# Two graph layers on one core: one block for both layers, closed blocks of new x among the last sums, and more rows fetched one by one

## The reference, cut to what matters

```python
h = maximum(layernorm(x), 0)
# layer 0: attention over the edges of each receiver, 4 heads of 32 channels
y = h @ W + b_lin
logit = leaky_relu(sum over (sent | received) channels of feat * alpha)   # per edge and head
att = exp(logit - max of the receiver) ; att = att / sum of the receiver
x = x + segment_sum(att * y[src], dst) + bias
h = maximum(layernorm(x), 0)
# layer 1: messages
ef  = (relu(edge_attr @ We1 + be1) @ We2 + be2) * sigmoid(ts @ Wt + bt)
msg = relu([h[src] | ef] @ Wn1 + bn1) @ Wn2 + bn2
x = x + (segment_sum(msg, dst) + h)
```

## Time and profile before

| | us |
|---|---|
| median of 3 runs (lowest, highest) | 2124.97 (2122.21, 2127.07) |
| the profiled execution's own time | 2122.82 |
| its span | 2121.0 |
| layer 0 from the start to the meeting of the engines | about 1055.7 |
| new x, to the first gather of layer 1 | 1055.7 to 1089.5 |
| layer 1 | 1089.5 to 2121.0 |

### The profile page before, as it was taken

The page is one execution under the profiler, slowest core; times in us unless marked ns, Lnnn a source line. Parts: engine busy times, 40 slices in busy tenths (PEclk is TensorE's granted clock), DMA queues, the critical chain, the costliest instruction groups (busy, mean ns, idle before and its releaser), DMA issues.

```text
span 2121.0 us, 47035 instructions
## 1 busy us (share of the span) xinstructions
PE 1524.8 (72%) x8785; PEld 1051.5 (50%) x8785; DVE 1461.3 (69%) x5237; ACT 929.9 (44%) x2818; POOL 1563.2 (74%) x1660
## 2 busy tenths in 40 slices
PE   6556555555555454454658998989989898898888
PEld 5434444444444343343545665656555555555556
DVE  8676767676766566565786886777767676666667
ACT  8535253535353342442466444444434443444343
POOL 7777777777777777777277777777777777777775
PEclk9766666666666666566679999999989999999999
DMA  7222222222222222222063544545544444454453
GB/s 203 54 57 57 57 57 57 58 57 57 57 58 57 56 58 57 57 56 54 22 184 107 144 144 144 145 123 146 150 128 144 144 145 144 119 146 138 133 151 105
DMA packets 111001, 213.56 MB, mean 101 GB/s; under 512 B 35214, under 2 KB 74350, under 8 KB 100723
## 3 DMA queue, kind: packets, MB, share of 16 engines
q0 software_dynamic: 51968, 107.32, 19.1%
q1 hardware_dynamic: 53031, 101.47, 16.2%
q10 hardware_dynamic: 5708, 1.77, 0.4%
HBM read 197.54 MB, written 12.88 MB: 99 GB/s over the span
## 4 chain that ended last, share of the span: by engine, by line
POOL 26%; issue 11%; PE 6%; DVE 5%; DMA 2%; ACT 1%; DVEq 1%; ACTq 0%; POOLq 0%; SPq 0%
POOL acc L1044 26%; DMA acc<-table,index 2%; PE pair L1122 1%; DVE acc L1392 1%; PE bank L1131 1%; PE pair L1116 1%; PE bank L1142 1%; DVE onehot L1350 1%; DVE pre L1374 1%; DVE ef L1357 1%; DVE x_rows L1288 0%; ACTq L1239 0%; PE bank L1073 0%; ACT msg L1223 0%; ACT hidden L1210 0%
## 5 line engine op out<-in xcount | busy, mean ns | idle before, releaser
L1044 POOL DMA_INDIRECT acc<-table,index x812 | 770.2, 949 | 252.5 <-issue 242.3
L356 POOL DMA_INDIRECT rows<-table,index x764 | 726.5, 951 | 233.0 <-issue 228.4
L812 ACT ACTIVATE rows<-rows,edge_w 128x32 f32<-128x32 f32 x1626 | 351.9, 313 | 1.1 <-issue 0.4
L504 DVE TENSOR_TENSOR acc<-acc,pair 128x256 f32 x832 | 349.2, 420 | 3.9 <-issue 2.5
L499 DVE TENSOR_SCALAR onehot<-iota_row,dst_rel 128x128 f32<-128x128 f32 x832 | 252.0, 304 | 135.2 <-PE pair L675 103.8
L1392 DVE TENSOR_TENSOR acc<-acc,bank 128x128 f32 x832 | 239.0, 287 | 143.5 <-issue 35.7
L675 PE MATMUL pair<-onehot,rows 128*128 128x128 f32 x1626 | 334.2, 367 | 0.5 <-ACT rows L812 0.5
L675 PEld LDWEIGHTS pair<-onehot,rows 128*128 128x128 f32 x1626 | 285.7, 264 | 58.9 <-issue 30.3
L1210 ACT ACTIVATE hidden<-pair,be 128x512 f32<-128x512 f32 x208 | 142.9, 687 | 380.0 <-PE pair L1122 172.4
L1131 PEld LDWEIGHTS bank<-wn1b,ef 128*128 128x128 f32 x1664 | 232.1, 202 | 109.7 <-issue 104.0
L1116 PE MATMUL pair<-ea,we 64*128 64x512 f32 x416 | 243.9, 668 | 42.4 <-DMA ea<-in_ea_t 42.4
(11 more groups left out here) (168 smaller groups left out, 1207.9 us busy)
## 6 DMA issues: line engine op xcount, KB each, us to landing
ts<-in_ts SPq DMA_DIRECT2D x52, 1024.0 KB
rows_x<-table SPq DMA_DIRECT2D x1664, 0.5 KB
ea<-in_ea_t SPq DMA_DIRECT2D x52, 512.0 KB, 5.0
rows_y<-table SPq DMA_DIRECT2D x1664, 0.5 KB
acc<-table,index POOLq DMA_INDIRECT x812
moments<-table ACTq DMA_DIRECT2D x768, 0.5 KB
rows_z<-table ACTq DMA_DIRECT2D x768, 0.5 KB
rows<-table,index POOLq DMA_INDIRECT x764
```

The source lines that it names most:

```text
L356: gp.indirect_dma_start(rows0[:, n % (RING * TG), :], None, table1, bass.IndirectOffsetOnAxis(index[:, n:n + 1], 0)).then_inc(half_in[g % ...
L504: dve.tensor_tensor(acc2[:, :, ds(v, P)], acc2[:, :, ds(v, P)], both_sums[n // TG % 2][:, :, n % TG * P:(n % TG + 1) * P], ALU.add).then_i ...
L812: act.activation(row, row, ACT.Copy, scale=edge_w[:, r % 2, (g - SPANS[r][0]) * TG + t, h:h + 1]).then_inc(scaled0, 1)
L1044: gp.indirect_dma_start(rows[:, g % RG1, t, :], None, table, bass.IndirectOffsetOnAxis(index[:, n:n + 1], 0)).then_inc(gathered[g % RG1], 16)
```

## The change

1. The two blocks become one: each engine runs its layer 0 program and goes on with its layer 1 program, without a meeting. The nodes are taken in the 13 parts that layer 1 closes them in (`CUTS`: one part per group from 195 on), in two stages: parts 0 to 8 (closed by group 203) and 9 to 12.
2. New x among the last sums: PE turns the statistics of closed parts during span 25 and the sums during span 26; DVE's statistics, shares, `scaled_sums` and `mix` stand between the last additions. POOL's own term now comes after `mix`, and SP writes a part to `table3` after the own term. PSUM banks 6 and 7 are freed for it (penalties, ends, carries and weights share bank 5). Tables of this step lie in slots of the ring of rows.
3. The maxima of span 26 are made within span 25 one group earlier (3, 4, 5, 6 for 4, 5, 6, 7). In every span `turn_penalties` stands after group 1 on PE and `keep_row_penalties` after group 2 on DVE (0 and 1 before).
4. SP fetches 15 tiles in layer 0 (groups 20, 33, ..., 189, a step of 13, and then 204) and the 10 rows of tile 830, for which `keep_logits` of span 26 waits too (`tail_in`); in layer 1 14 tiles (groups 21, 35, ..., 203, `LINE_STEP` 14) and the 10 rows of tile 830, ahead of the last `load`.
5. In SP's program the weights of layer 1 and `load(0)`, `load(1)` now come after the writes of `table3`.

The diff without the lines that only lose their indentation, cut:

```diff
-LINE_TILES = [g * TG for g in range(28, GROUPS, 14)]
-LINE_STEP = 15
+LINE_TILES = [g * TG for g in [*range(20, GROUPS - RG - HALF, 13), GROUPS - HALF]]
+LINE_STEP = 14
-EMPTY = range(-(-E // P), TILES)
+SHORT = E // P
+EMPTY = range(SHORT, TILES)
+LAST, CLOSE = TURNS - 1, TURNS - 2
+STAGES = [0, SPANS[LAST][0] - FIRST_END, PARTS]
...
-                return (4, 5, 6, 7) if r == TURNS - 1 else ()
+                return (3, 4, 5, 6) if r == LAST else ()
...
     # SyncE, layer 0
                     for j in range(len(LINE_TILES)):
                         line(j)
+                sp.wait_ge(agg0, SHORT // TG - RING + 1)
+                for o in range(0, E % P, BATCH):
+                    fill = min(BATCH, E % P - o)
+                    sp.load(regs[0:fill], line_index[0:1, len(LINE_TILES) * P + o:len(LINE_TILES) * P + o + fill])
+                    for q, v in enumerate(regs[0:fill]):
+                        row = sp.snap(v, min_val=0, max_val=N - 1)
+                        sp.dma_start(rows0[o + q:o + q + 1, SHORT % (RING * TG), :], table1[ds(row, 1), :]).then_inc(tail_in, 16)
                     sp.wait_ge(w2_in, 32)
+                for u in range(PARTS):
+                    sp.wait_ge(own, u + 1)
+                    sp.dma_start(table3[CUTS[u] * P:CUTS[u + 1] * P, :].rearrange("(b p) c -> p b c", p=P), x_rows[:, blocks_of(u), :]).then_inc(x1_out, 16)
...
     # ScalarE
                     def keep_logits(r):
+                    if r == LAST:
+                        act.wait_ge(tail_in, 16 * (E % P))
...
     # GpSimd, after the gathers of layer 0
+                for u in range(STAGES[1]):
+                    own_product(u)
+                for u in range(STAGES[1]):
+                    own_term(u)
+                for u in range(STAGES[1], PARTS):
+                    own_product(u)
+                for u in range(STAGES[1], PARTS):
+                    own_term(u)
...
     # VectorE, span 25 and then span 26
+                for k, g in enumerate(groups(CLOSE)):
+                    sum_group(g, at[k % HALF * TG:(k % HALF + 1) * TG])
+                    if k == logits_at:
+                        scan_rows(LAST)
+                    if k == ends_at:
+                        scan_row_ends(LAST)
+                    if k == carries_at:
+                        full_maxima(LAST)
+                    if k >= 1:
+                        gather_stats(k - 1)
+                gather_stats(7)
+                gather_stats(8)
+                maxima_of(0)
+                rescale(LAST, at)
+                shares(0)
+                sum_group(g1, at[0:TG])
+                scaled_sums(0)
+                sum_group(g1 + 1, at[TG:2 * TG])
+                scaled_sums(1)
+                mix(0)
+                add(n, at[2 * TG])
+                scaled_sums(2)
+                add(n + 1, at[2 * TG + 1])
+                mix(1)
...
+                gather_stats(12)
+                maxima_of(1)
+                scaled_sums(4)
+                shares(1)
+                scaled_sums(5)
+                mix(4)
...
+                scaled_sums(12)
+                mix(11)
+                mix(12)
...
     # SyncE, layer 1
+                def tail():
+                    sp.wait_ge(radd, SHORT // TG - RG1 + 1)
...
                     for q in range(loaded, GROUPS // HALF):
+                    if q == GROUPS // HALF - 1:
+                        tail()
                         load(q)
```

More of the change, by code:

```diff
@@ L22 @@
 UNITS = -(-NB // UB)
-EARLY = 3
 TG = 4
@@ L44 @@
 RAW_TURNS = 2
+WCOL = 4 * SH * (RT + 2)
+CARRY = WCOL + 2 * SH * (RT + 2)
 RAW = sum(SPAN_SIZES[:RAW_TURNS]) * TG
@@ L66 @@
 assert all(0 < y - x <= TG for x, y in zip(CUTS, CUTS[1:]))
+LAST, CLOSE = TURNS - 1, TURNS - 2
+STAGES = [0, SPANS[LAST][0] - FIRST_END, PARTS]
+assert STAGES == [0, 9, 13] and SPANS[CLOSE][1] == RG
+PART_SLOTS = 4
 ACT_ROWS = 4
@@ L234, in gnn_layers, with blocks_of, spread_of, heads @@
             act_index0_in = sem("act_index0_in")
+            sw_t, b_chain, e_in, e_done, s_t, cb_ready, ca_ready, owned, own, sums_kept, parted, mixed, count_kept, tail_in = (
+                sem(n) for n in ("sw_t", "b_chain", "e_in", "e_done", "s_t", "cb_ready", "ca_ready", "owned", "own", "sums_kept", "parted", "mixed",
+                                 "count_kept", "tail_in"))
+            def blocks_of(u):
+                return slice(CUTS[u], CUTS[u + 1])
+            def spread_of(u):
+                return CUTS[u + 1] - CUTS[u]
+            def heads(v):
+                return v.rearrange("p b (h c) -> p b h c", c=HC)
+            def per_head(v, u, n):
+                return v[:, blocks_of(u), 0:n].unsqueeze(3).broadcast_to([P, spread_of(u), n, HC])
+            def block_rows(b, u):
+                return b[:, 0:spread_of(u) * P].rearrange("p (m c) -> p m c", c=CH)
+            def stage(i):
+                return slice(CUTS[STAGES[i]], CUTS[STAGES[i + 1]])
+            def stage_of(u):
+                return next(i for i in range(2) if u < STAGES[i + 1])
+            turns_taken = ["t0", "t1", "t2", "t3", "t4", "t5", "t6", "t7", "t8", "s0", "s1", "s2", "s3", "t9", "t10", "t11", "t12",
+                           "s4", "s5", "s6", "s7", "s8", "s9", "s10", "s11", "s12"]
+            def stat_bank(u):
+                return bank[6 + turns_taken.index(f"t{u}") % 2]
+            def sum_bank(u):
+                return bank[6 + turns_taken.index(f"s{u}") % 2]
             def tiles(r):
@@ L848, in _ @@
                             keep_logits(r + 1)
+                    fetch(r)
+                    if r < CLOSE:
+                        keep_logits(r + 1)
+                shares_up(1)
         with ExitStack() as st:
-            sums_t = sb("sums_t", [P, NB, LCOL + SH], st=st)
-            top = sb("top", [P, NB, HEADS], st=st)
-            den = sb("den", [P, NB, HEADS], st=st)
-            parts = sb("parts", [P, 2, NB, HEADS], st=st)
             bn1_all = sb("bn1_all", [P, CH], st=st)
             wn1a = sb("wn1a", [P, CH], st=st)
-            part = sb("part", [P, 2, UB, CH], st=st)
@@ new lines, in second_gpsimd, with gather @@
+            def second_gpsimd(gp):
+                def gather(g, table):
+                    for t in range(TG):
+                        n = g * TG + t
+                        if n not in LINE_TILES1 and n not in ACT_TILES and n not in EMPTY:
+                            gp.indirect_dma_start(rows[:, g % RG1, t, :], None, table,
+                                                  bass.IndirectOffsetOnAxis(index[:, n:n + 1], 0)).then_inc(gathered[g % RG1], 16)
+                gp.wait_ge(x1_out, 16 * PARTS)
+                for g in range(RAW1):
+                    gather(g, table3)
+                for q in range(PROJ_SLOTS):
+                    gp.wait_ge(table1_out[q], 16 * len(range(q, UNITS, PROJ_SLOTS)))
+                for g in range(RAW1, GROUPS):
+                    if g >= RG1:
+                        gp.wait_ge(radd, g - RG1 + 1)
+                    gather(g, table2)
@@ new lines, in gnn_layers, with _ @@
+        with nc.Block() as block:
+            @block.gpsimd
+            def _(gp):
+                first_gpsimd(gp)
+                second_gpsimd(gp)
+            @block.scalar
+            def _(act):
+                first_scalar(act)
+                second_scalar(act)
+            @block.sync
+            def _(sp):
+                first_sync(sp)
+                second_sync(sp)
+            @block.tensor
+            def _(pe):
+                first_tensor(pe)
+                second_tensor(pe)
+            @block.vector
+            def _(dve):
+                first_vector(dve)
+                second_vector(dve)
```

1846 lines of the change are left out of this document (924 added, 922 removed).

## The result

The changed kernel takes 2185.59 us (median of 4 executions, 2184.17 to 2187.25), the kernel before 2123.89 (2122.21 to 2127.07) beside it on the same chip: a ratio of 1.0295, interval 1.0283 to 1.0308. The forecast was 2183. The profiled execution has a span of 2185.4, 64.4 more than before.

What follows compares the result with a forecast made beforehand. POOL's unbroken gathers, and SP's row fetches in program order, were taken to bound the kernel. First fetch 1159.3, to group 200 965.6 and the end 56.2 gave 2181.1 of span, forecast 2183 us; its own range 2158 to 2198, widened 2136 to 2198.

Steps and rivals of the forecast that it cites:

- What bounds the kernel: Whole kernel before: POOL's gathers never wait, but SP's row order also limits; SP has 100 us in hand in layer 0.
- Part 1: Layer 0, fifteen SP tiles: rows land at 1059.5, so span 26's logits turn at 1060.0 against 1029.50, +30.5 us.
- these cost nothing at the end: Layer 0, mid-layer tiles: spans 12 and 17 turn late, at 536 and 730, but are caught up; no cost at the end.
- Part 2: From span 26's logits turn to layer 1's first gather: 58.5 us, gather at 1118.5, -1.5 us.
- Part 3: Start of layer 1: later weights and loads put SP's first row fetch 40.8 us behind the first gather, at 1159.3.
- Part 4: Layer 1, fourteen SP tiles: group 200 begins 965.6 us after SP's first fetch against 938.9, +26.7; the stretch behind it -1.9.
- The sum: Whole kernel: 1159.3 + 965.6 + 56.2 = 2181.1 us of span, 2182.9 in own time, forecast 2183.
- A: Rival: late in layer 0 only, POOL sets layer 1's pace; 2149 us, up to 2153; chance 0.16.
- B: Rival: faster, SP's layer 0 rows come before POOL's last gather at 62.3 us a tile; 2115 us; chance 0.10.
- C: Rival: no change, late rows fall where DVE would have waited anyway; 2125 us; chance 0.03.
- The signs that I named: Between layers POOL stands some 65 us; it ends near 2134, almost 50 ahead; PE waits for `ea` at most multiples of four.

Runs made afterwards that it cites:

- the rewrite alone: The changed kernel with SP's tiles back at thirteen in both layers, the ten rows of tile 830 still SP's: 2121.72 us, ratio 0.9977.

## Why the prediction was right, step by step

**What bounds the kernel: right.** SP's issue order, hidden from the busy shares, had 100 us in hand in layer 0 and little in layer 1. The share of the chain on SP's queue says it, and moving one issue of each load shows it.

**Part 1: the number right, one sentence wrong.** The turn waited for SP's last rows, as forecast: ACT stood 13.1 us for them. They ended at 1056.6 (1057.4 forecast), the turn came at 1058.0 (1060.0), spans 12 and 17 turned at 536 and 730 as worked out. The pace of the spans that wait for nothing was 34.4 us, not 33. But "these cost nothing at the end" of the late tiles in the middle is false. Without the last tile the turn still came at 1049.9, 20.3 us late; the last tile adds 8.2. The last tile alone, with the middle on time, wasn't run, and since its rows and the ten behind it were out only at 1056.6, it would by my estimate have held the turn near 1058 by itself: the two overlap and don't add. I worked out spans 12 and 17 and stopped there. The same formula, 148.2 + 64.66 j, gives 859.5 for tile 11 in span 20 (858.8 measured), where the turn of before stood at 811.3, and I took the computation to catch up from there, being faster than POOL; five full spans at 34.4 us and the short last one end 20 us late. This is the sentence that failed. It did no harm to the number only because the last rows came later still.

**Part 2: right, the time 1.8 us shorter than forecast.** Turn to first gather 56.7 (58.5 forecast). The rewritten order is worth 4.4 to 4.7 us in the pairs with like tiles (55.6 against 60.0, and 56.7 against 61.4), where the sum gave it 1.5; over all traces it is 55.1 to 57.5 against 60.0 to 61.4. `mix` is 0.68 us alone and 0.90 beside POOL's own term; DVE's timeline of the kernel after:

```profile
1097.25 0.68 DVE L657 TENSOR_TENSOR x_rows<-x_rows,rows 128x512 f32<-128x512 f32 x1
...
1099.88 0.90 DVE L657 TENSOR_TENSOR x_rows<-x_rows,rows 128x512 f32<-128x512 f32 x1
```

**Part 3: right.** SP's first fetch 40.5 us behind the first gather (40.8 forecast), at 1155.3. In the rewrite alone it was 42.3, with 1.5 us of waiting for POOL.

**Part 4: the mechanism right, a term mis-sized.** `load(50)` came 966.35 us after SP's first fetch (960.3 forecast): 22.97 to the first gated load (25), then 943.4 (935.3) for 109 batches and 48 loads. I had a batch at 7.48 us and a load at 2.51. The 2.51 ran from the issue of `ea` to the next row. It held the issue of `ts` and some 1.4 us in which SP loads the registers of the next batch (here 1179.37 to 1180.82), which are part of every batch:

```profile
1178.79 0.58 SPq L1197 DMA_DIRECT2D ts<-in_ts  x1
1180.82 14.90 SPq L1205 DMA_DIRECT2D rows_y<-table  x32
```

Of the 48 stretches from one load to the next, 35 hold two batches and take 17.45 us on average, 13 hold three and take 25.59. So a batch is 8.14 us and a load 1.17. My pair gives 17.47 and 24.95: right for two batches, 0.64 us short for three, and 13 times that is 8.3 us, which covers the 8.1 that were missing. The seven stretches from which I took the pair held three batches only once, which is why it didn't show; with a step of 14 they do so more than twice as often as with 15 (13 against 6). From group 200 to the end 57.8 (56.2).

**The sum.** The errors are -2.0 in the turn, -1.8 and -0.3 up to SP's fetch, +6.8 to group 200, +1.6 behind it: +4.3, the 2185.4 against 2181.1. That 2183 came within 3 us of 2185.6 is partly luck: errors of -4.1 and +8.4 stood against each other.

**The rivals.** A (late in layer 0 only) fell: the run with 13 tiles in layer 0 kept 1.4%. B (SP fits) fell on 64.5 us a tile (968.0 / 15). C (hidden anyway) fell: the first gather is 25.3 us later. The signs that I named came, with these sizes: POOL stood 61.7 us until its own product (65 forecast) and ended at 2128.6 (2134), 56.8 us ahead of the kernel (almost 50), and PE waited for `ea` at 30 of the 52 groups that are multiples of four.

The Trainium skill, DMA: Bandwidth & Descriptors, "Issuing engines are not separate DMA queues", says that issuing from several engines saves only the issuer's time, which is "usually small relative to the DMA itself". The run with `ts` on ACT agrees: at equal bytes it took 0.55 us a load off SP, less than the 5.7 us in which an `ea` load lands in the kernel after. But it is 26.5 us over the layer, and the kernel became 27 us shorter. Small beside one DMA doesn't mean small for the kernel: here row fetches and the loads that gate the computation share one engine's program, and the sum of its issues decided.

## What to carry to other kernels

An engine whose program interleaves two kinds of work has two budgets: the total of its issues, and the position at which each gating load stands in the order. Work both out by position (start + pace x count against when the consumer needs it), not by comparing paces: being 2% faster doesn't mend a late start. Before taking a unit of work off the busy engine, set what it saves there (1.25 us a gather) against what it costs the helper (64.66 us a tile), and space it no closer than the helper's own time; at a step of fourteen groups the same fourteen tiles were free in layer 0. And follow late work through to the last place where it is late: an engine that is faster than the one it waits for takes back only a few us a span (39 against 34.4 here).

## What was not expected of the hardware

- A row of 0.5 KB fetched by its own DMA costs SP about 0.50 us with its share of the batch's register loads (968.0 / 1920), in layer 0 as in layer 1 (8.14 / 16), while POOL's indirect DMA brings 128 such rows for 1.25 us.
- The issue of one `ts` (a broadcast load of 1 MB) took SP 0.58 us (above, at 1178.79) and ACT 0.37 us:

```profile
1182.10 0.37 ACTq L1414 DMA_DIRECT2D ts<-in_ts  x1
```
